# The first layer's triangle: row blocks outside, channels inside, with b kept on chip in fp16 parts

## The chip, the core and the metric

The kernel runs on one core of a Trainium2 chip. The metric is device time in microseconds (us) of one execution. TensorE (PE in the profile; PEld its weight loads), VectorE (DVE), ScalarE (ACT), GpSimd (POOL) and SyncE (SP, which here only issues DMAs) run their own instruction streams, each in order; they wait for each other by semaphores.

## The reference, cut to what matters

The input x is a pair tensor of 512 x 512 x 128, fp32. Two layers follow each other; both are residual and begin with a group normalisation. The change lies in the first layer:

```
a = sigmoid((x @ Wa1 + ba1) * (x @ Wa2 + ba2))        # 512 x 512 x 16
b = sigmoid((x @ Wb1 + bb1) * (x @ Wb2 + bb2))        # 512 x 512 x 16
g = sigmoid(x @ Wg + bg)
z = einsum('bikc,bkjc->bijc', a, b)                   # 16 products of 512 x 512 matrices
x = x + g * (layernorm(z over c) @ Wz + bz)
```

So each of the 16 channels c is one matrix product z[:, :, c] = a[:, :, c] @ b[:, :, c], and the layer norm then runs over the 16 channels of each pair (i, j). The second layer has a similar pair of triangles and is not touched.

## The kernel before

There are seven stages behind each other with a barrier between them: statistics, gates (writes a and b to the DRAM tensor ab_d, as [512, 32, 512] fp32), the triangle (stage 3, changed here), the first layer's output, and three stages of the second layer. Stage 3 reads ab_d and writes the normalised z as two fp16 parts (rounded value and rest) to z_d.

The products are made in fp16 parts: a value is the sum of high (the value rounded to fp16, by ScalarE) and rest (value minus high, by VectorE). One product of a row block of 128 rows i with all 512 columns j is 12 matmuls: 4 blocks of the sum index k, times three terms (high x high, high x rest, rest x high).

The channels are the outer loop and the four row blocks `ib` the inner one. Per channel, SyncE loads all of a[c] and all of b[c] (1 MB each) into a ring of three `raw` buffers (L617): the next a waits until a buffer's transposes are done, the next b until a buffer's rests are done. TensorE transposes a (`turn`, L637, four transposes of 128x128 for each of four units into `t_ps`). ScalarE makes high from `t_ps` and from `raw` (L670), VectorE makes rest (L733), both into `ab`, which has two buffers, so that channel c + 1 is prepared during the products of channel c. The lists ORDER and AFTER fix by hand in which order the 8 units of the next channel are placed between the products. TensorE's 12 matmuls write `z_ps` (L649). ScalarE copies channel 0 to `z` (L691); for the other channels VectorE subtracts channel 0 while it copies (`take`, L748). Channel 0 so serves as a base that makes the values small; its own slot is zeroed later. GpSimd adds up z (L722) and the squares that ScalarE makes (L678, L726) in `total` and `total2`.

After the last channel come, for each row block, the variance (L752, L755), the square root (L699), the zeroing (L759) and the reciprocal (L761), and then for each half of 8 channels: normalising (L767, VectorE), rounding (L705, ScalarE), the rest (L771, VectorE) and two stores of 1 MB (L621, L623). All of that stands behind the last product.

Of the kernel before, what the change touches and what calls it, by code (L numbers as in the profile page):

```python
# [11 lines left out]
P = 128  # L12
# [561 lines left out]
def stage3_triangle(nc, K, ab_d, z_d, N):  # L574
# [4 lines left out]
    RB, C, SLOTS = N // P, 16, 3  # L579
    UNITS, CHUNK = 2 * RB, C // 2  # L580
    AFTER = ((4, 5), (0, 1, 6), (2, 3, 7), ())
    ORDER = (4, 5, 0, 1, 6, 2, 3, 7)
    a_v = ab_d.rearrange("(b p) c k -> c p b k", p=P)
    b_v = ab_d.rearrange("(p b) c k -> c p b k", b=RB)
    z_v = z_d.rearrange("(h c) (b p) j -> h b p c j", h=2, p=P)
    with ExitStack() as stack:
        s = Scope(nc, stack, "s3")
        raw = s.sbuf("raw", [P, SLOTS, RB, N])
        ab = s.sbuf("ab", [P, 2, 2, 2, RB, N], FP16)
        z = s.sbuf("z", [P, C, RB, N])  # L590
        total, total2 = s.sbuf("total", [P, RB, N]), s.sbuf("total2", [P, RB, N])
        parts = ab[:].rearrange("p x m h k j -> p (x m h k) j").rearrange("p (x h c) j -> p x h c j", x=2, h=2)
        def square(c, n):

            return z[:, C - 1, 2 + n % 2, :] if c + 1 < C else raw[:, 2, n % 2, :]

        z_ps = s.psum("z_ps", [P, RB, BANK])
        t_ps = s.psum("t_ps", [P, 4, BANK])
        loaded, stored = s.sems("loaded", SLOTS), s.sems("stored", 2)
        turned, rounded, rest_ready, product, taken, squared, summed, summed2 = [  # L600
            s.sem(n) for n in ("turned", "rounded", "rest_ready", "product", "taken", "squared", "summed", "summed2")]
        zeroed, meant, scaled, var_ready, dev_ready, inverted, cleared, normed, z_rounded, z_split = [
            s.sem(n) for n in ("zeroed", "meant", "scaled", "var_ready", "dev_ready", "inverted", "cleared", "normed", "z_rounded", "z_split")]

        @block_of(nc)
        def _(block):
            @block.sync
            def _(sp):
                for n in range(2 * C):
                    c, m = n // 2, n % 2  # L610
                    before = n - SLOTS
                    if before >= 0 and before % 2 == 0:
                        sp.wait_ge(turned, RB * (before // 2 + 1))
                    elif before >= 0:
                        sp.wait_ge(rest_ready, UNITS * (before // 2 + 1))
                    src = (a_v[c], b_v[C + c])[m]
                    sp.dma_start(raw[:, n % SLOTS, :, :], src).then_inc(loaded[n % SLOTS], 16)  # L617
                for k in range(2 * RB):
                    ib, half = k // 2, slice(CHUNK * (k % 2), CHUNK * (k % 2) + CHUNK)
                    sp.wait_ge(z_rounded, k + 1)  # L620
                    sp.dma_start(z_v[0, ib][:, half, :], parts[:, k % 2, 0, :, :]).then_inc(stored[k % 2], 16)  # L621
                    sp.wait_ge(z_split, k + 1)
                    sp.dma_start(z_v[1, ib][:, half, :], parts[:, k % 2, 1, :, :]).then_inc(stored[k % 2], 16)  # L623
                for k in range(2):
                    sp.wait_ge(stored[k], RB * 32)

            @block.tensor
            def _(pe):
                def turn(c, q):

                    n = 2 * c
                    if q == 0:
                        pe.wait_ge(loaded[n % SLOTS], n // SLOTS * 16 + 16)
                    if c:
                        pe.wait_ge(rest_ready, UNITS * (c - 1) + ORDER.index(q) + 1)
                    for b in range(RB):
                        last = pe.transpose(t_ps[:, q, b * P:(b + 1) * P], raw[:, n % SLOTS, b, q * P:(q + 1) * P], K.ident[:])  # L637
                    last.then_inc(turned, 1)

                for q in range(RB):  # L640
                    turn(0, q)
                for c in range(C):
                    pe.wait_ge(rest_ready, UNITS * (c + 1))
                    for ib in range(RB):
                        if c:
                            pe.wait_ge(taken, RB * (c - 1) + (ib + 1))
                        terms = [(kb, a, b) for kb in range(RB) for a, b in ((0, 0), (0, 1), (1, 0))]
                        for m, (kb, a, b) in enumerate(terms):
                            last = pe.matmul(z_ps[:, ib, 0:N], ab[:, c % 2, 0, a, kb, ib * P:(ib + 1) * P], ab[:, c % 2, 1, b, kb, :],  # L649
                                             start=m == 0, stop=m == len(terms) - 1)  # L650
                        last.then_inc(product, 1)
                        if c + 1 < C and ib + 1 < RB:
                            for v in AFTER[ib + 1]:
                                if v < RB:
                                    turn(c + 1, v)

            @block.scalar
            def _(act):
                def round_high(c, v):
                    if c >= 2 and v == ORDER[0]:  # L660
                        act.wait_ge(product, RB * (c - 1))
                    if v < RB:
                        act.wait_ge(turned, RB * c + v + 1)
                        src = t_ps[:, v, 0:N]
                    else:
                        n = 2 * c + 1
                        if v == RB:
                            act.wait_ge(loaded[n % SLOTS], n // SLOTS * 16 + 16)
                        src = raw[:, n % SLOTS, v % RB, :]
                    act.activation(ab[:, c % 2, v // RB, 0, v % RB, :], src, ACT.Copy).then_inc(rounded, 1)  # L670

                def take_square(c, ib):

                    n = RB * (c - 1) + ib
                    act.wait_ge(taken, RB * c + ib + 1)
                    if n >= 2:
                        act.wait_ge(summed2, n - 1)
                    act.activation(square(c, n), z[:, c, ib, :], ACT.Square).then_inc(squared, 1)  # L678

                for v in ORDER:  # L680
                    round_high(0, v)
                for c in range(C):
                    for ib in range(RB):
                        if c + 1 < C:
                            for v in AFTER[ib]:
                                round_high(c + 1, v)
                        if c and ib:
                            take_square(c, ib - 1)
                        if c == 0:
                            act.wait_ge(product, ib + 1)  # L690
                            act.activation(z[:, 0, ib, :], z_ps[:, ib, 0:N], ACT.Copy).then_inc(taken, 1)  # L691
                    if c:
                        take_square(c, RB - 1)
                for ib in range(RB):
                    act.wait_ge(summed, RB * (C - 2) + ib + 1)
                    act.wait_ge(summed2, RB * (C - 1) - 1 + ib // 2)
                    act.activation(raw[:, 0, ib, :], total[:, ib, :], ACT.Square, scale=1.0 / C).then_inc(meant, 1)
                    act.wait_ge(var_ready, ib + 1)
                    act.activation(raw[:, 1, ib, :], total2[:, ib, :], ACT.Sqrt).then_inc(dev_ready, 1)  # L699

                def round_z(k):
                    act.wait_ge(normed, k + 1)
                    if k >= 2:
                        act.wait_ge(stored[k % 2], k // 2 * 32)
                    act.activation(parts[:, k % 2, 0, :, :], z[:, CHUNK * (k % 2):CHUNK * (k % 2) + CHUNK, k // 2, :],  # L705
                                   ACT.Copy).then_inc(z_rounded, 1)

                for k in range(2 * RB):
                    round_z(k)

            @block.gpsimd
            def _(pool):
                pool.memset(total[:], 0.0).then_inc(zeroed, 1)  # L713
                pool.memset(total2[:], 0.0).then_inc(zeroed, 1)
                pool.wait_ge(zeroed, 2)
                for c in range(1, C):
                    for ib in range(RB):
                        n = RB * (c - 1) + ib
                        pool.wait_ge(taken, RB * c + ib + 1)
                        if c > 1:  # L720
                            pool.wait_ge(summed, n - 3)
                        pool.tensor_tensor(total[:, ib, :], total[:, ib, :], z[:, c, ib, :], ALU.add).then_inc(summed, 1)  # L722
                        pool.wait_ge(squared, n + 1)
                        if c > 1:
                            pool.wait_ge(summed2, n - 3)
# [1117 lines left out]
```

## Time and profile before

| | us |
|---|---|
| median of 3 runs (4824.75 to 4827.78) | 4825.3 |
| the profiled execution | 4827.47 |
| its span, first to last instruction | 4825.7 |
| TensorE / VectorE / ScalarE / GpSimd busy in the span | 3997.2 / 3925.1 / 3395.2 / 2674.1 |

The granted TensorE clock is 0.975 in the mean over the span (1.00 is 2.4 GHz, 0.50 is 1.2 GHz). Stage 3 issues its first load at 943.45 us of the span, and stage 4 starts at 1254.05. A row of the view by groups reads: line, engine, operation, written tile <- read tiles, shapes, count | busy us in the stretch, mean ns of one | idle time of the engine before them, and what ended it. A row in order of time reads: start us, us, engine, line, what, and in square brackets the idle time before it.

### The profile page before, as it was taken

The page shows a single profiled execution, that of the slowest core. Times are in us where ns is not written, and L with a number is a line of the kernel's source. Part 1 is how long each engine was busy: PE and PEld are TensorE (multiplying, and loading weights), DVE is VectorE, ACT ScalarE, POOL GpSimd, SP SyncE. Part 2 cuts the span into 40 slices and gives each one's busy share as a digit, 9 for nine tenths or more (in the row PEclk, how much of TensorE's full clock was granted, in tenths as well). Part 3 has the DMA queues.
Part 4 walks back from the last instruction along what each step waited for, and adds up shares of the span by engine and source line. Part 5 has one row for each costly group of instructions (what it writes and reads, how often), then busy time and mean ns, then how long its engine had stood idle before and what let it go on. Part 6 is the DMA issues. An engine that isn't in the chain of part 4 may idle for free. (4 is left out here: it accounts for less than half of the span.)

```text
span 4825.7 us, 89597 instructions
## 1 busy us (share of the span) xinstructions
PE 3997.2 (83%) x26438; PEld 2240.6 (46%) x26438; DVE 3925.1 (81%) x5450; ACT 3395.2 (70%) x4840; POOL 2674.1 (55%) x1428
## 2 busy tenths in 40 slices
PE   0007888795599999889999999979999978888888
PEld 0004444452366666545555555545554434444444
DVE  5787777678888888989999999867779987777777
ACT  2337777654577777768888888746667768888887
POOL 0000000085488888757778777843334418888887
PEclk9999999997799999989999999999999989999999
DMA  9997888753999999969999999876679869999999
GB/s 367 416 385 247 296 299 301 241 175 105 307 399 390 390 391 391 393 215 316 315 315 318 311 313 318 276 263 222 224 237 308 302 213 362 407 405 404 402 404 362
DMA packets 700625, 1532.70 MB, mean 318 GB/s; under 512 B 32976, under 2 KB 50832, under 8 KB 698128
## 3 DMA queue, kind: packets, MB, share of 16 engines
q1 hardware_dynamic: 563696, 1263.31, 73.0%
q10 hardware_dynamic: 136864, 268.59, 14.5%
q8 instruction: 33, 0.54, 0.0%
q14 instruction: 32, 0.26, 0.0%
HBM read 1009.59 MB, written 522.19 MB: 317 GB/s over the span
## 5 line engine op out<-in xcount | busy, mean ns | idle before, releaser
L1762 POOL TENSOR_TENSOR s_oT<-s_gated,s7in_x1t 128x1024 f32<-128x1024 f32 x256 | 689.4, 2699 | 218.5 <-DVE s_gated L1681 213.6
L976 POOL TENSOR_TENSOR s_x1T<-s_gz,s_xT 128x512 f32<-128x512 f32 x512 | 653.4, 1276 | 126.6 <-DVE s_gz L942 122.0
L1428 PE MATMUL s_y_ps<-s_ab 128*128 128x512 f16 x3072 | 678.4, 379 | 1.8 <-DVE s_ab L1499 1.8
L1133 POOL TENSOR_TENSOR s_low<-s_xc,s_high 128x1024 f16<-128x1024 f32 x256 | 547.8, 2140 | 237.4 <-ACT s_high L1094 235.9
L873 PE MATMUL s_g_ps<-s_xT,s_Wg 128*128 128x512 f32 x1024 | 523.3, 593 | 0.0
L713 POOL MEMSET s_total<- 128x2048 f32 x1 | 1.8, 1810 | 936.2 <-POOLq L41 936.2
L903 ACT ACTIVATE s_g<-s_g_ps,s_bg 128x512 f32<-128x512 f32 x512 | 352.0, 688 | 173.1 <-PE s_g_ps L873 173.1
L1681 DVE SCALAR_TENSOR_TENSOR s_gated<-s_p_ps,k_po_bias,s_gate 128x1024 f32<-128x1024 f32 x256 | 328.7, 1284 | 177.2 <-ACT s_gate L1718 145.7
L1428 PEld LDWEIGHTS s_y_ps<-s_ab 128*128 128x128 f16 x3072 | 300.4, 98 | 343.4 <-issue 2.0
L548 DVE SCALAR_TENSOR_TENSOR s_low<-s_x_ps,k_gn_scale,s_high 128x1024 f16<-128x1024 f32 x256 | 328.5, 1284 | 161.0 <-ACT s_high L498 160.9
L942 DVE SCALAR_TENSOR_TENSOR s_gz<-s_z_ps,k_z_bias,s_g 128x512 f32<-128x512 f32 x512 | 384.4, 751 | 88.8 <-ACT s_g L903 86.6
L1099 ACT ACTIVATE s_gate<-s_g_ps,k_gi_bias 128x1024 f32<-128x1024 f32 x256 | 284.3, 1110 | 200.7 <-PE s_g_ps L1268 200.4
L1402 POOL TENSOR_TENSOR s_at<-s_at,s_mask 128x1024 f32<-128x1024 f32 x64 | 151.1, 2360 | 460.6 <-DMA s_bt<-h_d 265.6
L1718 ACT ACTIVATE s_gate<-s_g_ps,k_go_bias 128x1024 f32<-128x1024 f32 x256 | 286.0, 1117 | 148.0 <-PE s_g_ps L1627 134.8
L863 PEld LDWEIGHTS s_x_ps<-k_ident,s_xt 128*128 128x128 f32 x2048 | 257.1, 141 | 274.8 <-issue 268.3
L1172 DVE BATCH_NORM_STATS2 s_stats<-s_x_ps 128x6 f32<-128x256 f32 x1024 | 364.1, 418 | 7.8 <-PE s_x_ps L1243 7.1
L1201 DVE SCALAR_TENSOR_TENSOR s_h<-s_p_ps,k_pi_bias,s_gate 128x1024 f32<-128x1024 f32 x256 | 328.2, 1282 | 46.8 <-PE s_p_ps L1268 32.2
L933 DVE BATCH_NORM_STATS2 s_stats<-s_x1T 128x512 f32 (+1 forms) x512 | 349.8, 683 | 0.2 <-POOL s_x1T L976 0.2
L498 ACT ACTIVATE s_high<-s_x_ps,k_gn_scale 128x1024 f16<-128x1024 f32 x256 | 285.2, 1114 | 74.3 <-PE s_x_ps L454 73.6
L307 DVE BATCH_NORM_STATS2 s_stats<-s_xt 128x512 f32 x416 | 248.5, 682 | 81.1 <-DMA s_xt<-in_x 81.1
L863 PE MATMUL s_x_ps<-k_ident,s_xt 128*128 128x128 f32 x2048 | 308.5, 274 | 6.5 <-DVE s_bg L929 6.5
L1194 DVE TENSOR_TENSOR s_xc<-s5in_xt,s_r_ps 128x1024 f32<-128x1024 f32 x256 | 310.2, 1212 | 4.3 <-PE s_r_ps L1259 3.0
(225 smaller groups left out, 9506.7 us busy)
## 6 DMA issues: line engine op xcount, KB each, us to landing
s2in_xt<-in_x SPq DMA_DIRECT2D x128, 1024.0 KB, 8.5
s_xt<-in_x SPq DMA_DIRECT2D x256, 512.0 KB, 8.4
x_d<-s_x1T ACTq DMA_DIRECT2D x128, 1024.0 KB, 9.6
s5in_xt<-x_d SPq DMA_DIRECT2D x128, 1024.0 KB, 9.2
h_d<-s_h SPq DMA_DIRECT2D x128, 1024.0 KB, 6.9
s7in_x1t<-x_d SPq DMA_DIRECT2D x128, 1024.0 KB, 14.0
out<-s_ot ACTq DMA_DIRECT2D x128, 1024.0 KB, 9.3
s_mask_b<-mask_d SPq DMA_DIRECT2D x128, 512.0 KB, 4.8
```

The lines of the kernel that those rows point to most:

```text
L548: dve.scalar_tensor_tensor(low[:, g % GROUPS, 2 * h:2 * h + 2, :], x_ps[:, (2 * g + h) % SLOTS, :, 0:N], K.gn_scale[:], high[:, g % GROUPS ...
L863: last = pe.transpose(x_ps[:, i % 4, q * P:(q + 1) * P], xt[:, i // U, i % U, q, :], K.ident[:])
L873: pe.matmul(g_ps[:, i % 2, 0:N], Wg[:], xT[:, i % 8, :], start=True, stop=True).then_inc(g_prod, 1)
L903: act.activation(g[:, i % 2, :], g_ps[:, i % 2, 0:N], ACT.Sigmoid, bias=bg[:]).then_inc(sig, 1)
L933: dve.bn_stats(stats[:, bass.ds(r * ROWS + i, 1), :].rearrange("p a s -> p (a s)"), x1T[:, i // U, i % U, :]).then_inc(counted, 1)
L942: dve.scalar_tensor_tensor(gz[:, i % 4, :], z_ps[:, i % 2, 0:N], K.z_bias[:], g[:, i % 2, :], ALU.add, ALU.mult).then_inc(mixed, 1)
L976: pool.tensor_tensor(x1T[:, i // U, i % U, :], gz[:, i % 4, :], xT[:, i % 8, :], ALU.add).then_inc(added, 1)
L1133: pool.tensor_tensor(low[:, n % 4, :, :], xc[:, n % 4, :, :], high[:, n % 4, :, :], ALU.subtract).then_inc(rest_ready, 1)
L1172: last = dve.bn_stats(stats[:, row // 16 % 2, row % 2, row // 2 % BLOCK, a, :], x_ps[:, row % 2, 2 * a * P:(2 * a + 2) * P].rearrange("p ( ...
L1428: last = pe.matmul(y_ps[:, ib, 0:N], ab[:, u % 2, 0, a, kb, ib * P:(ib + 1) * P], ab[:, u % 2, 1, b, kb, :], start=m == 0, stop=m == len(t ...
L1681: dve.scalar_tensor_tensor(gated[:, n % 4, :, :], p_ps[:], K.po_bias[:], gate[:, n % 2, :, :], ALU.add, ALU.mult).then_inc(mixed, 1)
L1762: pool.tensor_tensor(oT[:, n % 4, :, :], gated[:, n % 4, :, :], x1t[:, n // 2, 2 * (n % 2):2 * (n % 2) + 2, :], ALU.add).then_inc(added, 1)
```

## The change

The loops are exchanged: the row block n of 128 rows is the outer loop and the channel c the inner one, 64 steps g = 16 n + c. All 16 channels of b are loaded, rounded and kept in fp16 parts (`b`) during block 0; a is loaded in pieces of 128 rows of one channel (256 KB), three deep. `z` becomes a ring of 24 slots of one block and channel; the landing place of b, `raw_b`, is in the eight slots that block 0 doesn't use. Block n is normalised in chunks of two channels during the channels of block n + 1 (the steps are in the tables NORM, ROUND and SPLIT), the last block after the last product. The normalising reads the reciprocal deviation from PSUM (`dev_ps`). There is one `square`, `total` and `total2` buffer of one block in place of one for each block, and GpSimd starts each block's sums with copies instead of adding to zeroed tiles. The diff is cut to what each engine issues in which order:

```diff
+    RB, C, ZS, CHUNK, TERMS = N // P, 16, 24, 2, ((0, 0), (0, 1), (1, 0))
+    CHUNKS, LATER, STEPS = C // CHUNK, C - 1, RB * C
+    NORM, ROUND, SPLIT = (4, 5, 7, 8, 10, 11, 13, 14), (5, 6, 8, 9, 11, 12, 14, 15), (6, 7, 9, 10, 12, 13, 15, 16)
...
+        b = s.sbuf("b", [P, C, 2, RB, N], FP16)
+        raw_a = s.sbuf("raw_a", [P, 3, N])
+        a = s.sbuf("a", [P, 3, 2, N], FP16)
+        z = s.sbuf("z", [P, ZS, N])
+        raw_b = z[:, C:C + 2 * RB, :].rearrange("p (s b) j -> p s b j", b=RB)
+        square = s.sbuf("square", [P, N])
+        z_ps = s.psum("z_ps", [P, 3, BANK])
+        t_ps = s.psum("t_ps", [P, 3, BANK])
...
             def _(sp):
+                for g in range(STEPS):
+                    if g < C:
+                        if g >= 2:
+                            sp.wait_ge(b_rest, g - 1)
+                        sp.dma_start(raw_b[:, g % 2, :, :], b_v[C + g]).then_inc(b_loaded[g % 2], 16)
+                    if g >= 3:
+                        sp.wait_ge(turned, g - 2)
+                    sp.dma_start(raw_a[:, g % 3, :], a_v[g // C, g % C]).then_inc(a_loaded[g % 3], 16)
+                    for n, k in due(g - 6, SPLIT):
+                        store(n, k)
...
             def _(pe):
+                for g in range(STEPS):
+                    if g + 2 < STEPS:
+                        turn(g + 2)
+                    pe.wait_ge(a_rest, g + 1)
+                    pe.wait_ge(b_rest, min(g, C - 1) + 1)
+                    before = g - 3
+                    if before >= 0 and before % C == 0:
+                        pe.wait_ge(based, before // C + 1)
+                    elif before >= 0:
+                        pe.wait_ge(taken, later(before))
...
             def _(act):
+                def round_b(c):
+                    act.wait_ge(b_loaded[c % 2], c // 2 * 16 + 16)
+                    act.activation(b[:, c, 0, :, :], raw_b[:, c % 2, :, :], ACT.Copy).then_inc(b_rounded, 1)
...
+                round_b(0)
+                for g in range(2):
+                    round_a(g)
+                for g in range(STEPS):
+                    n, c = g // C, g % C
+                    if g + 2 < STEPS:
+                        round_a(g + 2)
+                    if g + 1 < C:
+                        round_b(g + 1)
+                    if c == 0:
+                        take_base(g)
+                    if g and (g - 1) % C:
+                        take_square(g - 1)
+                    if n and c == 1:
+                        mean_square(n - 1)
+                    if n and c == 2:
+                        deviation(n - 1)
+                    for block_n, k in due(g, ROUND):
+                        round_z(block_n, k)
...
             def _(dve):
+                def normalize(n, k):
+                    dve.wait_ge(inverted, n + 1)
+                    dve.wait_ge(cleared, n + 1)
+                    part = chunk_of(n, k)
+                    dve.tensor_tensor(part, part, dev_ps[:, 0:N].rearrange("p (a j) -> p a j", a=1).to_broadcast([P, CHUNK, N]), ALU.mult).then_inc(normed, 1)
...
+                rest_b(0)
+                for g in range(2):
+                    rest_a(g)
+                for g in range(STEPS):
+                    n, c = g // C, g % C
+                    if g + 2 < STEPS:
+                        rest_a(g + 2)
+                    if g + 1 < C:
+                        rest_b(g + 1)
+                    if c:
+                        take(g)
+                    if n and c == 1:
+                        variance(n - 1)
+                    if n and c == 2:
+                        clear_base(n - 1)
+                    if n and c == 3:
+                        invert(n - 1)
+                    for block_n, k in due(g, SPLIT):
+                        split(block_n, k)
+                    for block_n, k in due(g, NORM):
+                        normalize(block_n, k)
...
-        K.gn_mean, K.gn_scale, K.gn_shift = s.sbuf("gn_mean", [P, 1]), s.sbuf("gn_scale", [P, 1]), s.sbuf("gn_shift", [P, 1])
+        columns = s.sbuf("gn", [P, 4])
+        K.gn_mean, K.gn_scale, K.gn_shift = columns[:, 0:1], columns[:, 1:2], columns[:, 2:3]
```

In it, `turn(g)` waits for a_loaded of g, for rest_a(g - 3) and transposes; `round_a(g)` waits for turn(g) and for product g - 3; `rest_a` and `rest_b` wait for the rounding of the same piece; `take(g)` waits for product g; `store` waits for z_rounded and z_split of its chunk, and `round_z(j)` for the two stores of chunk j - 2. GpSimd's two adds of step g wait for `taken` and `squared` of that step, and `take_square(g)` for the add of the square before.

## Rows read from the trace of the kernel before

**Rows 1.** Busy time by stretch: us, busy and count by engine, clock, DMA share, GB/s.
```profile
965.00:1147.00 182.00, 182.00 (x960) 97.30 (x959) 138.53 (x175) 98.19 (x177) 157.97 (x112) 1.00 0.49 157
...
1163.00:1254.00 91.00, 0.00 (x0) 0.00 (x0) 83.54 (x24) 29.13 (x9) 0.00 (x0) 0.50 0.55 185
```
**Rows 2.** Busy time by stretch, one channel in the middle of stage 3.
```profile
1051.00:1063.10 12.10, 12.10 (x65) 6.51 (x64) 9.98 (x14) 7.10 (x13) 11.56 (x8) 1.00 0.54 173
```
**Rows 3.** Order of time, start of stage 3.
```profile
943.45 51.77 SPq L617 DMA_DIRECT2D s_raw<-ab_d  x11
...
951.00 3.68 PE L637 MATMUL s_t_ps<-k_ident,s_raw 128*128 128x128 f32 x16 [13.18 <-DMA s_raw<-ab_d]
953.68 1.15 ACT L670 ACTIVATE s_ab<-s_raw 128x512 f16<-128x512 f32 x2 [14.38 <-DMA s_raw<-ab_d]
...
959.30 4.10 PE L649 MATMUL s_z_ps<-s_ab 128*128 128x512 f16 x12 [4.62 <-DVE s_ab L733]
```
**Rows 4.** Order of time, the last take, the last store, and stage 4's start.
```profile
1152.86 0.69 DVE L748 TENSOR_TENSOR s_z<-s_z_ps,s_z 128x512 f32<-128x512 f32 x1 [1.90 <-PE s_z_ps L649]
...
1246.73 0.37 SPq L623 DMA_DIRECT2D z_d<-s_ab  x1
1254.05 6.92 POOL L968 MEMSET s_zt<- 64x8192 f16 x1 [96.50 <-POOLq L41]
```
**Rows 5.** SyncE's waits in stage 3: us in total, times, longest us.
```profile
SPq L617 <- PE s_t_ps L637: 126.8, 15, 9.6
...
SPq L617 <- DVE s_ab L733: 39.6, 14, 4.0
```
**Rows 6.** Transfers: line 617's landings, then others (count, KB, median us to landing).
```profile
DMA to landing us min/median/max: 5.2/5.7/11.7
...
z_d<-s_ab SPq DMA_DIRECT2D x16, 1024.0 KB, 4.5
s_mask<-mask_d SPq DMA_DIRECT2D x1, 512.0 KB, 4.0
...
k_Wg<-in_Wg SPq DMA_DIRECT2D x1, 64.0 KB, 2.0
```
**Rows 7.** Busy time by stretch, PE alone, in the first transposes: clock, DMA, GB/s last.
```profile
951.00:952.00 1.00, 1.00 (x5) 0.50 1.04 393
```
**Rows 8.** Groups of instructions by line and shape, 930 to 1260 us.
```profile
L722 POOL TENSOR_TENSOR s_total<-s_total,s_z 128x512 f32<-128x512 f32 x60 | 78.2, 1303 | 41.1 <-DVE s_z L748 41.0
...
L733 DVE TENSOR_TENSOR s_ab<-s_raw,s_ab 128x512 f16<-128x512 f32 x64 | 73.1, 1162 | 37.1 <-ACT s_ab L670 37.1
L748 DVE TENSOR_TENSOR s_z<-s_z_ps,s_z 128x512 f32<-128x512 f32 x60 | 41.0, 683 | 25.7 <-PE s_z_ps L649 25.7
L733 DVE TENSOR_TENSOR s_ab<-s_t_ps,s_ab 128x512 f16<-128x512 f32 x64 | 40.8, 677 | 4.8 <-ACT s_ab L670 4.8
...
L678 ACT ACTIVATE s_z<-s_z 128x512 f32<-128x512 f32 x56 | 35.4, 632 | 61.7 <-DVE s_z L748 61.5
L767 DVE TENSOR_TENSOR s_z<-s_z,s_total 128x4096 f32<-128x4096 f32 x8 | 34.9, 4409 | 0.0
L771 DVE TENSOR_TENSOR s_ab<-s_z,s_ab 128x4096 f16<-128x4096 f32 x8 | 34.9, 4401 | 0.0
...
L670 ACT ACTIVATE s_ab<-s_t_ps 128x512 f16<-128x512 f32 x64 | 34.7, 594 | 14.8 <-PE s_t_ps L637 14.7
...
L705 ACT ACTIVATE s_ab<-s_z 128x4096 f16<-128x4096 f32 x8 | 28.9, 3618 | 49.6 <-DVE s_z L767 49.6
L761 DVE RECIPROCAL s_total<-s_raw 128x512 f32<-128x512 f32 x4 | 13.2, 3294 | 0.0
```
**Rows 9.** Line 733 reading SBUF, 965 to 1147 us: duration ns min/median/max.
```profile
L733 DVE TENSOR_TENSOR s_ab<-s_raw,s_ab x58: 681/1186/1792, 965.8 to 1139.9; 128x512 f16<-128x512 f32 x58
```
**Rows 10.** Order of time, VectorE and GpSimd near 1127 us.
```profile
1126.79 1.27 POOL L722 TENSOR_TENSOR s_total<-s_total,s_z 128x512 f32<-128x512 f32 x1
1127.41 1.19 DVE L733 TENSOR_TENSOR s_ab<-s_raw,s_ab 128x512 f16<-128x512 f32 x1
1128.02 1.73 POOL L726 TENSOR_TENSOR s_total<-s_total,s_z 128x512 f32<-128x512 f32 x1
```

More of the change, by code:

```diff
@@ L584, in stage3_triangle @@
     b_v = ab_d.rearrange("(p b) c k -> c p b k", b=RB)
-    z_v = z_d.rearrange("(h c) (b p) j -> h b p c j", h=2, p=P)
+    z_v = z_d.rearrange("(h c) (n p) j -> h n p c j", h=2, p=P)
     with ExitStack() as stack:
         s = Scope(nc, stack, "s3")
[L588 to L603, printed above, removed]
@@ L605, in _, with later, chunk_of, due @@
+        normed, z_rounded, z_split = s.sem("normed"), s.sem("z_rounded"), s.sem("z_split")
+        def later(g):
+            return LATER * (g // C) + g % C
+        def chunk_of(n, k):
+            first = (C * n + CHUNK * k) % ZS
+            return z[:, first:first + CHUNK, :]
+        def due(step, table):
+            return [(step // C - 1 - e, k) for e in (0, 1) for k, at in enumerate(table)
+                    if at == step % C + C * e and 0 <= step // C - 1 - e < RB - 1]
         @block_of(nc)
@@ L608, in _ @@
             def _(sp):
[L609 to L625, printed above, removed]
+                def store(n, k):
+                    j = CHUNKS * n + k
+                    channels = slice(CHUNK * k, CHUNK * k + CHUNK)
+                    for h, ready in ((0, z_rounded), (1, z_split)):
+                        sp.wait_ge(ready, j + 1)
+                        sp.dma_start(z_v[h, n][:, channels, :],
+                                     parts[:, j % 2, h, :, :]).then_inc(stored[j % 2], 16)
@@ L627, in _ @@
+                for step in range(STEPS - 6, STEPS + 1):
+                    for n, k in due(step, SPLIT):
+                        store(n, k)
+                for k in range(CHUNKS):
+                    store(RB - 1, k)
+                for x in range(2):
+                    sp.wait_ge(stored[x], RB * CHUNKS // 2 * 32)
             @block.tensor
             def _(pe):
[L629 to L637, printed above, removed]
-                    last.then_inc(turned, 1)
@@ L640, in _, with turn @@
[L640 to L655, printed above, removed]
+                def turn(g):
+                    pe.wait_ge(a_loaded[g % 3], g // 3 * 16 + 16)
+                    if g >= 3:
+                        pe.wait_ge(a_rest, g - 2)
+                    for q in range(RB):
+                        last = pe.transpose(t_ps[:, g % 3, q * P:(q + 1) * P], raw_a[:, g % 3, q * P:(q + 1) * P], K.ident[:])
+                    last.then_inc(turned, 1)
@@ new lines, in _ @@
+                for g in range(2):
+                    turn(g)
+                for g in range(STEPS):
[8 more added lines that the diff above has]
+                        pe.wait_ge(taken, later(before))
+                    terms = [(q, x, y) for q in range(RB) for x, y in TERMS]
+                    for m, (q, x, y) in enumerate(terms):
+                        last = pe.matmul(z_ps[:, g % 3, 0:N], a[:, g % 3, x, q * P:(q + 1) * P], b[:, g % C, y, q, :],
+                                         start=m == 0, stop=m == len(terms) - 1)
+                    last.then_inc(product, 1)
@@ L657, in _ @@
             @block.scalar
             def _(act):
[L659 to L670, printed above, removed]
@@ L694, in _ @@
[L694 to L706, printed above, removed]
@@ L708, in _, with round_a @@
-                for k in range(2 * RB):
-                    round_z(k)
+                def round_a(g):
+                    act.wait_ge(turned, g + 1)
+                    if g >= 3:
+                        act.wait_ge(product, g - 2)
+                    act.activation(a[:, g % 3, 0, :], t_ps[:, g % 3, 0:N], ACT.Copy).then_inc(a_rounded, 1)
+                def round_b(c):
+                    act.wait_ge(b_loaded[c % 2], c // 2 * 16 + 16)
+                    act.activation(b[:, c, 0, :, :], raw_b[:, c % 2, :, :], ACT.Copy).then_inc(b_rounded, 1)
@@ new lines, in take_base, with take_square @@
+                def take_base(g):
+                    n = g // C
+                    act.wait_ge(product, g + 1)
+                    if n == 1:
+                        act.wait_ge(b_rest, C)
+                    if n >= 2:
+                        act.wait_ge(z_split, CHUNKS * (n - 2) + (ZS - C) // CHUNK + 1)
+                    act.activation(z[:, g % ZS, :], z_ps[:, g % 3, 0:N], ACT.Copy).then_inc(based, 1)
+                def take_square(g):
+                    m = later(g)
+                    act.wait_ge(taken, m)
+                    if m >= 2:
+                        act.wait_ge(summed2, m - 1)
+                    act.activation(square[:], z[:, g % ZS, :], ACT.Square).then_inc(squared, 1)
@@ L711, in _ @@
+                take_square(STEPS - 1)
+                mean_square(RB - 1)
+                deviation(RB - 1)
+                for k in range(CHUNKS):
+                    round_z(RB - 1, k)
             @block.gpsimd
             def _(pool):
[L713 to L725, printed above, removed]
-                        pool.tensor_tensor(total2[:, ib, :], total2[:, ib, :], square(c, n), ALU.add).then_inc(summed2, 1)
+                for g in range(STEPS):
+                    n, c, m = g // C, g % C, later(g)
+                    if c == 0:
+                        continue
+                    pool.wait_ge(taken, m)
+                    if c == 1:
+                        if n:
+                            pool.wait_ge(meant, n)
+                        pool.tensor_copy(total[:], z[:, g % ZS, :]).then_inc(summed, 1)
+                        pool.wait_ge(squared, m)
+                        if n:
+                            pool.wait_ge(dev_ready, n)
+                        pool.tensor_copy(total2[:], square[:]).then_inc(summed2, 1)
+                    else:
+                        pool.wait_ge(summed, m - 1)
+                        pool.tensor_tensor(total[:], total[:], z[:, g % ZS, :], ALU.add).then_inc(summed, 1)
+                        pool.wait_ge(squared, m)
+                        pool.wait_ge(summed2, m - 1)
+                        pool.tensor_tensor(total2[:], total2[:], square[:], ALU.add).then_inc(summed2, 1)
@@ L774, in _, with rest_a @@
-                for ib in range(RB):
-                    variance(ib)
-                for ib in range(2):
-                    invert(ib)
-                for ib in range(RB):
-                    normalize(2 * ib)
-                    normalize(2 * ib + 1)
-                    if ib + 2 < RB:
-                        invert(ib + 2)
-                    split(2 * ib)
-                    split(2 * ib + 1)
+                def rest_a(g):
+                    dve.wait_ge(a_rounded, g + 1)
+                    dve.tensor_tensor(a[:, g % 3, 1, :], t_ps[:, g % 3, 0:N], a[:, g % 3, 0, :], ALU.subtract).then_inc(a_rest, 1)
@@ new lines, in rest_b, with take @@
+                def rest_b(c):
+                    dve.wait_ge(b_rounded, c + 1)
+                    dve.tensor_tensor(b[:, c, 1, :, :], raw_b[:, c % 2, :, :], b[:, c, 0, :, :], ALU.subtract).then_inc(b_rest, 1)
+                def take(g):
+                    n = g // C
+                    dve.wait_ge(product, g + 1)
+                    dve.wait_ge(based, n + 1)
+                    if g >= ZS:
+                        dve.wait_ge(z_split, (g - ZS) // CHUNK + 1)
+                    elif n:
+                        dve.wait_ge(b_rest, C)
+                    dve.tensor_tensor(z[:, g % ZS, :], z_ps[:, g % 3, 0:N], z[:, C * n % ZS, :], ALU.subtract).then_inc(taken, 1)
@@ new lines, in split @@
+                def split(n, k):
+                    j = CHUNKS * n + k
+                    dve.wait_ge(z_rounded, j + 1)
+                    dve.tensor_tensor(parts[:, j % 2, 1, :, :], chunk_of(n, k), parts[:, j % 2, 0, :, :], ALU.subtract).then_inc(z_split, 1)
+                rest_b(0)
+                for g in range(2):
+                    rest_a(g)
+                for g in range(STEPS):
+                    n, c = g // C, g % C
[15 more added lines that the diff above has]
+                        normalize(block_n, k)
@@ L787, in stage4_layer0 @@
+                for block_n, k in due(STEPS, SPLIT):
+                    split(block_n, k)
+                last = RB - 1
+                variance(last)
+                clear_base(last)
+                invert(last)
+                normalize(last, 0)
+                for k in range(1, CHUNKS):
+                    normalize(last, k)
+                    split(last, k - 1)
+                split(last, CHUNKS - 1)
 def stage4_layer0(nc, K, x, z_d, x1_d, N, ahead):
```

99 lines of the change are left out of this document (37 added, 62 removed).

## The prediction

> **What bounds the kernel now.** The change touches one stage, the first layer's triangle. I read the busy time by stretch first. From 965 to 1147 us TensorE is busy for all of it, while from 1163 to 1254 it does nothing and VectorE is busy for 83.54 of 91 us [rows 1]. So the stage has two parts with two limits: 16 channels at TensorE's pace, then a normalising tail at VectorE's pace. The stretch of one channel gives the pace of the first part: 12.10 us, four row blocks of 12 matmuls and 4 transposes, so 3.02 us for one block of one channel [rows 2]. The order of time gives the ends: the last "take" (VectorE subtracting the base from z_ps) starts at 1152.86, the last store is issued at 1246.73 and stage 4 starts at 1254.05 [rows 4]. SyncE issues the first load at 943.45 [rows 3], so the stage takes 310.6 us, and 101.2 of it lie behind the last take's start.
>
> **What the change removes.** TensorE's work is the same: 64 steps of 12 matmuls and 4 transposes. The tail shrinks, because three of four blocks are normalised beside the next block's products. What is new is the pace of the first block, in which all 16 channels of b must be loaded (1 MB each), rounded and kept.
>
> **Block 0, the term that decides.** I write t(c) for the end of VectorE's rest_b(c). Follow the four queues; each is in order.
> - SyncE, turn g: it waits for rest_b(g-2), issues the 1 MB load of b(g), and only then the 256 KB load of a(g). That it stands still for VectorE is nothing new: it did so 14 times before, for up to 4.0 us [rows 5]; but now the load of a is behind that wait.
> - TensorE, step g-2: turn(g) comes first, so it waits for a(g).
> - ScalarE, step g-2: round_a(g), then round_b(g-1). The second is queued behind the first, although b(g-1) landed long ago.
> - VectorE, step g-2: rest_a(g), then rest_b(g-1).
>
> So t(g-1) cannot come before t(g-2) + the load of b(g) and a(g) + turn(g) + round_a(g) + round_b(g-1) + rest_b(g-1), for g = 2 to 15. The three-deep ring for a and the two-deep ring for b hide nothing: each step pays a whole load. The price of one round:
> - Loads. A 1 MB load of this tensor lands 5.2 us after its issue at best, 5.7 in the median [rows 6]; queued loads follow at 2.7 us per MB (the first consumer starts at 951.00, the second load's at 953.68) [rows 3], which is 0.7 for 256 KB. 5.2 to 5.7 and 0.7, with 0.1 for SyncE to wake: 6.3 us (6.0 to 6.9).
> - turn(g): 16 transposes took 3.68 us in a stretch whose granted clock was 0.50, the lower of the two levels [rows 3, 7], so 0.92 for 4. In block 0 TensorE idles most of a step, so I take this; at the upper level it would be half, 0.46.
> - round_a: 0.59 [rows 8].
> - round_b, 2048 elements: between 0.632 for 512 and 3.618 for 4096 [rows 8] lies a slope of 0.833 ns per element, so 1.91.
> - rest_b, 2048 elements: between 0.681 for 512 undisturbed [rows 9] and 4.401 for 4096 [rows 8], slope 1.038, so 2.28. rest_a (0.68) runs beside round_b, the products beside the load.
> - Handing over between engines: 0.1.
>
> Sum 6.3 + 0.9 + 0.6 + 1.9 + 2.3 + 0.1 = 12.1 us a round, bounds 10.6 (5.2 for the loads, with a(g) landing 0.2 behind b(g), 0.46 for the turn, no handing over) and 13.2 (6.9 for the loads, and half an add of GpSimd in the way, 0.5). GpSimd's adds fall into the load's time, so I charge no wait here. TensorE alone would want 3.02.
>
> A page speaks on the load term. The Trainium skill (DMA: Bandwidth & Descriptors, section "Anatomy of one DMA — SWDGE (gpsimd) path") gives a fit of 2.0 us fixed plus bytes over 436 GB/s. For 1.25 MB that is an estimate of 5.0 us; the rows have 5.2 for 1 MB alone. By the page a round would be 1.3 shorter and the time about 18 us less; the rows decide.
>
> Start of the block: b(0) is now first in the queue and lands at 951.0 as the first load did; 1.9 + 2.3 later t(0) = 955.2, 11.8 us after the stage's start. Fourteen rounds, 169.4 us, lead to t(14). a(16) and a(17) wait for no b, so rest_b(15) is done 4 to 5 us after t(14), beside matmul(14): that is 4.1 us at the low clock [rows 3], turn(17) 0.5, matmul(15) 2.6 (3.02 less a turn): 7.2 us to the end of product 15.
>
> **Blocks 1 to 3.** TensorE wants 16 x 3.02 = 48.4 us a block. VectorE's count: 16 x (rest_a 0.677 + take 0.683) = 21.8 [rows 8]; three short operations at 0.68 = 2.0; one reciprocal 3.29 [rows 8]; 8 normalisings and 8 splits of 1024 elements, 0.681 + 512 x 1.038 ns = 1.21 each, 19.4 (before: 4.4 for 4096 either way [rows 8]). Sum 46.5, no lower bound on the time since TensorE's 48.4 is above it. On top come waits for GpSimd. The row pair of VectorE and GpSimd shows them: a subtraction with both inputs in SBUF, started at 1127.41, took 1.19 and ended 0.54 after GpSimd's add ended at 1128.06; GpSimd's next add, started at 1128.02, took 1.73 in place of 1.27 [rows 10]. They take turns. The subtraction that reads PSUM has a mean of 0.677 beside the same adds, that from SBUF 1.162 [rows 8]. So rest_a, take and normalising (one input in PSUM) pay nothing, and the 8 splits do: from nothing to a whole add of 1.27, hence a block between 48.4 and 46.5 + 10.2 = 56.7. GpSimd is nearly full itself: 15 pairs of adds at 1.27 are 38.1, with 8 splits that shut it out 47.8, so half an add, 0.6, is the value nearest to the row: 46.5 + 4.8 = 51.3, and I take 51. Three blocks: 153 us (145 to 168). Three banks of z_ps let VectorE fall two steps behind, so uneven steps (the one with the reciprocal) average out. Loads of a and stores of parts are issued some three steps ahead, 9 us, against landings of 2.0 for 64 KB, 4.0 for 512 KB and 4.5 for 1 MB [rows 6]; they are covered. ScalarE has 16 x (0.594 + 0.632) + 8 x 1.06 + 2.4, about 31 of 51 us.
>
> **The tail.** After product 63: take 0.7, GpSimd's last adds (some behind, so up to 5 us; at least 0.63 for the square and 1.27 for an add), variance 1.4, Sqrt 0.65, reciprocal 3.3: about 10. Then 8 chunks of normalise and split at 2.42: 19.4, or up to 23, since round_z waits for the stores of two chunks before; I take 21. From the last store's issue to stage 4 it was 7.3 with 1 MB at 4.5, so 2.8 beside the landing [rows 4, 6]; 256 KB between 2.0 and 4.0 gives about 6. Tail 37 (31 to 40).
>
> **Sum.** 11.8 + 169.4 + 7.2 + 153 + 37 = 378.4 us in place of 310.6: 68 us more. The profiled execution took 4827.5 us, so 4895.4 by its own time; the median of the runs is 2.2 lower, so 4893. The bounds: 11.8 + 148 + 6 + 145 + 31 = 342 gives +31 (4857); 11.8 + 185 + 8 + 168 + 40 = 413 gives +102 (4927). The stages behind read z_d in the same layout and start when the stage ends; I charge them nothing. The three gn columns cut from one tile are read by the same instructions: nothing.
>
> **Rivals.**
> - *Block 0 runs at the pace of VectorE and GpSimd, and the kernel is faster.* If the loads ran ahead, a step would cost rest_b 2.28 plus a pair of adds 2.54 that take turns with it, 4.8 us. 14 x (4.8 - 12.1) = -102, so 34 us under before: 4791. For it: 393 GB/s while loads are queued [rows 7], so the data themselves want 3.4 us a step. Against it: SyncE's queue held loads behind VectorE in the kernel before too [rows 5], and the load of a stands behind that wait in the code. The point from which it decides: a round below 12.1 - 68/14 = 7.2 us, for which the loads would have to cost 1.4. Chance 4%.
> - *a(g) doesn't wait for the bytes of b(g).* Then it lands as a 256 KB load by itself, about 2.9 us between the rows' 2.0 and 4.0 [rows 6], 0.6 after b's issue; a round is 9.4 and the time 68 - 38 = 30 us above before: 4855. Against it: the first two loads landed 2.7 us apart [rows 3]. Chance 9%. The Trainium skill (DMA: Bandwidth & Descriptors, "Queues, rings and completion order") says that completion is not in order per issuing engine, which would allow this; the same section lets each engine take descriptors in ring order, which the rows' 2.7 us agree with.
> - *VectorE and GpSimd bind blocks 1 to 3.* At 56.7 a block, 17 us more: 4910. For it: GpSimd's 47.8 of 48.4. Against it: five of eight splits have a step without normalising behind them, to catch up. Chance 12%.
> - *The loss in block 0 and the gain in the tail cancel*: within 0.2% (9.7 us, about what a measurement of this kernel can tell from no change), which wants a round near 7.2. Chance 2%.
>
> **How the numbers follow.** Forecast 73%, the rivals 4, 9, 12 and 2%. The likeliest time is 4893. The range takes in the second and third rival and the bounds: 4852 to 4928. Faster 0.04, same 0.02, slower 0.94.
>
> **What would show it.** In the changed profile: rest_b of neighbouring channels 12 us apart in block 0; TensorE idle there for some 60% of the time, its transposes waiting for the DMA of raw_a about 6 us, 14 times; ScalarE's round_a waiting for TensorE as often; a low granted clock there; after it steps of 3.0 to 3.3 us; splits well above 1.21 in the mean and normalisings at 1.2; about 37 us from the last product to stage 4. Wrong: rest_b starts 5 us apart, SyncE not waiting for VectorE, or TensorE's steps in blocks 1 to 3 above 3.6 us.

## The result and the profile after

The changed kernel takes 4876.65 us in the median of 4 runs (4876.49 to 4876.76); the kernel before took 4825.97 beside it. The ratio is 1.0103, with a 95% interval of 1.009 to 1.0116: 50.7 us slower. The forecast was 4893, with 4852 to 4928 as its range.

The busy time by stretch shows where. The columns are those of [rows 1]: the stretch and its length, busy us and count of PE, PEld, DVE, ACT and POOL, granted clock, DMA share, GB/s. The stretches are the 14 rounds of block 0, then blocks 1, 2 and 3, then what follows the last product. Blocks 1 to 3 are each counted from the start of their second product; the first three products behind the rounds, from 1120.54 to 1131.19, lie in no stretch.

```profile
955.03:1120.54 165.51, 76.60 (x232) 34.46 (x232) 50.65 (x44) 41.07 (x43) 46.53 (x24) 0.66 0.34 116
1131.19:1179.60 48.41, 48.41 (x258) 26.25 (x257) 43.97 (x49) 28.70 (x44) 41.69 (x30) 1.00 0.53 156
1179.60:1228.00 48.40, 48.40 (x258) 26.24 (x257) 46.18 (x52) 27.29 (x43) 43.95 (x31) 1.00 0.59 175
1228.00:1272.40 44.40, 44.40 (x231) 23.26 (x229) 42.19 (x48) 23.67 (x37) 40.04 (x28) 1.00 0.49 150
1272.40:1307.88 35.48, 0.00 (x1) 0.00 (x0) 28.61 (x24) 12.28 (x14) 7.42 (x5) 0.55 0.44 148
```

In block 0 no engine is busy for half of the time and the DMA engines have a share of 0.34: nothing is full, so it is a chain of waits. In blocks 1 to 3 TensorE is busy for all of it, beside the normalising of the block before. The tail behind the last product is 35.5 us; before, 101.2 us lay behind the last take's start. The stage's first load and stage 4's start:

```profile
945.47 0.65 SPq L634 DMA_DIRECT2D s_z<-ab_d  x1
...
1307.88 6.92 POOL L1031 MEMSET s_zt<- 64x8192 f16 x1 [28.06 <-POOLq L41]
```

So the stage takes 362.4 us.

One round of block 0 in order of time (start us, us, engine, line, what; in brackets the idle time before it and what ended it):

```profile
966.84 0.55 SPq L634 DMA_DIRECT2D s_z<-ab_d  x1
967.43 0.62 SPq L637 DMA_DIRECT2D s_raw_a<-ab_d  x1
972.69 0.71 PEld L655 LDWEIGHTS s_t_ps<-k_ident,s_raw_a 128*128 128x128 f32 x4 [6.90 <-DMA s_raw_a<-ab_d]
...
973.60 3.69 PE L672 MATMUL s_z_ps<-s_b,s_a 128*128 128x512 f16 x12
973.85 0.60 ACT L682 ACTIVATE s_a<-s_t_ps 128x512 f16<-128x512 f32 x1 [6.92 <-PE s_t_ps L655]
974.34 1.90 ACT L686 ACTIVATE s_b<-s_z 128x2048 f16<-128x2048 f32 x1
974.48 0.69 DVE L774 TENSOR_TENSOR s_a<-s_t_ps,s_a 128x512 f16<-128x512 f32 x1 [7.66 <-ACT s_a L682]
976.27 2.29 DVE L778 TENSOR_TENSOR s_b<-s_z,s_b 128x2048 f16<-128x2048 f32 x1 [1.11 <-ACT s_b L686]
...
978.59 0.55 SPq L634 DMA_DIRECT2D s_z<-ab_d  x1
```

(`raw_b` lies in `z`, so the load of b is `s_z<-ab_d`.) From the issue of b(g) to the next one it is 11.75 us: 5.85 until a(g) has landed and its turn starts, 1.16 for the turn up to round_a's start, 0.49 to round_b's start, 1.93 to rest_b's start, 2.29 for rest_b, and SyncE issues the next b at once. The first rest_b starts at 952.74, the fifteenth at 1118.25: 14 rounds of 11.82. SyncE's waits (us in total, times, longest) answer to [rows 5]; 14 waits for rest_b have grown from 39.6 to 144.6 us:

```profile
SPq L634 <- DVE s_b L778: 144.6, 14, 10.7
SPq L637 <- PE s_t_ps L655: 85.1, 38, 4.7
```

### The profile page after: what moved, and what is told of

Same layout as the page of the kernel before. It is cut to its first block and busy times, and to the rows that moved or that the text cites. A ratio compares the mean times of both kernels' runs of the same rounds, so it can differ in the third digit from the quotient of the medians.

```text
span 4875.0 us, 89868 instructions
## 1 busy us (share of the span) xinstructions
PE 4023.5 (83%) x26438; PEld 2249.4 (46%) x26438; DVE 3904.5 (80%) x5450; ACT 3393.9 (70%) x4816; POOL 2688.9 (55%) x1426
## 5 line engine op out<-in xcount | busy, mean ns | idle before, releaser
L548 DVE SCALAR_TENSOR_TENSOR s_low<-s_x_ps,k_gn,s_high 128x1024 f16<-128x1024 f32 x256 | 328.5, 1283 | 161.1 <-ACT s_high L498 161.1
L498 ACT ACTIVATE s_high<-s_x_ps,k_gn 128x1024 f16<-128x1024 f32 x256 | 285.2, 1114 | 74.9 <-PE s_x_ps L454 74.8
```

## The experiments

Theory: in block 0 the load of a(g) stands in SyncE's queue behind the wait for rest_b(g-2), while ScalarE and VectorE have round_b(g-1) and rest_b(g-1) queued behind a(g). So each channel pays one load and all that follows it, one after the other. The rival is that the loads, or the work of the engines itself, need that time in any order.

**SyncE's order: a(g) ahead of b(g)'s wait** (e1_a_first)

```diff
+                    if g >= 3:
+                        sp.wait_ge(turned, g - 2)
+                    if g >= 2:
+                        sp.dma_start(raw_a[:, g % 3, :], a_v[g // C, g % C]).then_inc(a_loaded[g % 3], 16)
                     if g < C:
                         if g >= 2:
                             sp.wait_ge(b_rest, g - 1)
                         sp.dma_start(raw_b[:, g % 2, :, :], b_v[C + g]).then_inc(b_loaded[g % 2], 16)
...
```

> Only SyncE's order is changed: from g = 2 the load of a(g) is issued ahead of the wait for rest_b(g-2) and of the load of b(g). My theory (a round of block 0 is one chain, because the load of a(g) is queued behind the wait for rest_b(g-2), so that each round pays load 5.9, turn 1.15, round_a 0.5, round_b 1.9 and rest_b 2.3, 11.8 in all): a(g) is then behind rest_b(g-3), the same chain spans two channels, rest_b starts 5.9 us apart, and the kernel takes 4876.7 - 14 x 5.9 = 4794 us, which is also less than before. Rival (the round is the work of the engines and of the loads, which has to be done in any order): rounds above 10 us and 4860 or more.

Measured: 4796.66 us, ratio to before 0.9941 (0.9924 to 0.9957). The 16 rest_b start from 953.01 to 1042.60, 5.97 us apart. The view of their line (count: duration ns min/median/max, first and last start):

```profile
L781 DVE TENSOR_TENSOR s_b<-s_z,s_b x16: 2291/2292/2294, 953.0 to 1042.6; 128x2048 f16<-128x2048 f32 x16
```

The chain is right in kind and in size (5.9 expected), and the same amount of work and bytes takes half the time once two instructions have changed places.

**ScalarE's and VectorE's order: b(g+1) ahead of a(g+2)** (e2_b_first)

```diff
-                    if g + 2 < STEPS:
-                        round_a(g + 2)
                     if g + 1 < C:
                         round_b(g + 1)
+                    if g + 2 < STEPS:
+                        round_a(g + 2)
...
                     if g + 1 < C:
                         rest_b(g + 1)
+                    if g + 2 < STEPS:
+                        rest_a(g + 2)
```

> SyncE's order stays; ScalarE does round_b(g+1) ahead of round_a(g+2) and VectorE rest_b(g+1) ahead of rest_a(g+2). My theory: rest_b(g-1) no longer stands behind a(g); the chain closes over two channels (load 5.9, turn 1.15, round_a 0.6, a square 0.6, round_b 1.9, rest_b 2.3 = 12.4), 6.2 us a round, 4876.7 - 14 x 5.6 = 4798 us: nearly the same as the edit of SyncE's order, from the other end of the chain. Rival (the chain closes elsewhere, in SyncE's own queue or in the loads): rounds of 10 us or more and 4855 or more.

Measured: 4811.86 us, ratio 0.9967 (0.9954 to 0.9979). The chain opens from this end too, but rounds are 6.84 us in the mean (952.90 to 1055.51), not 6.2. They come in pairs, 3.4 and 10.4. VectorE and TensorE in order of time in the long one:

```profile
991.41 1.12 PE L655 MATMUL s_t_ps<-k_ident,s_raw_a 128*128 128x128 f32 x4 [6.11 <-DMA s_raw_a<-ab_d]
992.32 4.10 PE L672 MATMUL s_z_ps<-s_b,s_a 128*128 128x512 f16 x12
...
996.46 0.69 DVE L788 TENSOR_TENSOR s_z<-s_z_ps,s_z 128x512 f32<-128x512 f32 x1 [2.58 <-PE s_z_ps L672]
997.06 2.28 DVE L778 TENSOR_TENSOR s_b<-s_z,s_b 128x2048 f16<-128x2048 f32 x1
```

In this order rest_b stands behind the take of the step before, and that waits for a product that is itself behind the turn of a(g) and takes 4.10 us (the granted clock from 991.41 to 996.46 is 0.64; at 1.00 a product takes 2.75). round_b had ended at 995.47, so the detour over TensorE costs some 1.6 us in each pair. I had left the take out of this chain.

**SyncE's order, one more step: a(g+1) ahead of b(g)'s wait** (e3_a_ahead)

```diff
...
+                    elif g < C:
+                        if g == 2:
+                            load_a(2)
+                        load_a(g + 1)
+                        sp.wait_ge(b_rest, g - 1)
+                        sp.dma_start(raw_b[:, g % 2, :, :], b_v[C + g]).then_inc(b_loaded[g % 2], 16)
...
```

> SyncE's order alone, one more step ahead: a(g+1) is issued ahead of the wait for rest_b(g-2) and of the load of b(g). My theory: a is out of the chain; what is left is the two-deep ring of b (load 5.2, round_b 1.9, rest_b 2.3 = 9.5 for two channels, 4.8 a round), beside VectorE's rest_b and GpSimd's two adds, which take turns (2.24 + 2.44 = 4.7): rounds of 4.8 to 5.3, 4876.7 - 14 x 6.8 = 4782 (4775 to 4788). Rival (a's place in the queue is not what counts; b's ring alone sets the round in the first edit too): no faster than that one, 4790 to 4800.

Measured: 4782.81 us, ratio 0.9911 (0.9895 to 0.9928): 43 us less than before, and the fastest of the kernels that leave nothing out. rest_b starts 5.01 us apart (951.89 to 1027.11):

```profile
L787 DVE TENSOR_TENSOR s_b<-s_z,s_b x16: 2292/2293/2689, 951.9 to 1027.1; 128x2048 f16<-128x2048 f32 x16
```

**Both loads behind the wait, a(g) first** (e4_same_wait)

```diff
                     if g < C and g >= 2:
                         sp.wait_ge(b_rest, g - 1)
...
                     sp.dma_start(raw_a[:, g % 3, :], a_v[g // C, g % C]).then_inc(a_loaded[g % 3], 16)
+                    if 2 <= g < C:
+                        sp.dma_start(raw_b[:, g % 2, :, :], b_v[C + g]).then_inc(b_loaded[g % 2], 16)
...
```

> a(g) still waits for rest_b(g-2), but is issued ahead of b(g) instead of behind it. My theory: the chain stays, its load is a(g) alone, 2.9 us as in blocks 1 to 3 in place of 5.9, so rounds of 8.8 us and 4876.7 - 14 x 3.0 = 4835 us. Rival (bytes of b in front of a don't count, since loads of one queue share the engines): a lands about 5 us after its issue, rounds above 11 us, 4868 or more.

Measured: 4830.35 us, ratio 1.0012 (1.0003 to 1.0022). Rounds of 8.48 us (953.42 to 1072.07 in 14). In order of time, a round's loads and the turn that waits for them:

```profile
981.40 0.33 SPq L637 DMA_DIRECT2D s_raw_a<-ab_d  x1
981.78 0.55 SPq L639 DMA_DIRECT2D s_z<-ab_d  x1
...
984.19 0.66 PE L657 MATMUL s_t_ps<-k_ident,s_raw_a 128*128 128x128 f32 x4 [4.03 <-DMA s_raw_a<-ab_d]
```

2.8 us from a's issue to its use, with 1 MB of b right behind it; in the changed kernel, with b in front, it is 5.26 from a's issue and 5.85 from b's. The place behind b's bytes and the wait are two parts of the chain: without b in front a round is 3.3 us shorter (8.48 against 11.82; 3.0 had been expected), and with a ahead of the wait too, as in the first edit, another 2.5 (5.97).

**Each split of blocks 0 to 2 made twice** (e5_split_twice)

```diff
                     for block_n, k in due(g, SPLIT):
+                        spare(block_n, k)
+                        dve.wait_ge(spared, CHUNKS * block_n + k + 1)
                         split(block_n, k)
...
```

(`spare` is the same subtraction into the same tile.)

> The changed kernel with each split of blocks 0 to 2 (during blocks 1 to 3) made twice by VectorE, the second over the first. My theory: these blocks run at TensorE's pace, 48.4 us, but VectorE has only some 2 us idle in each, so that 8 more splits of 1.13 to 2.3 us (the wait for GpSimd's adds included) make VectorE the bound: 7 to 16 us more per block, 4898 to 4925 us in all. Rival (VectorE is far from the bound and its waits would fill with the extra work): under 4882.

Measured: 4913.63 us, 37 us above the changed kernel (ratio to before 1.0177, 1.016 to 1.0194). Its block 2, from the last take of block 1 to its own last take, by the view by stretch:

```profile
1193.49:1253.12 59.63, 49.64 (x253) 25.73 (x252) 59.27 (x60) 27.21 (x43) 49.58 (x31) 0.98 0.48 142
```

VectorE is busy for 59.27 of 59.63 us: with 8 more splits it is the bound, 11.2 us above TensorE's 48.4. They added 13.1 us to VectorE's busy time (46.18 in the changed kernel's block 2) and 11.2 to the block. So the changed kernel had some 2 us of room on VectorE in each block, and no more.

**What holds the better order at 5 us a round.** Two suspects lay at nearly one height: the ring of b (load, round_b and rest_b of a slot, two channels deep) and VectorE taking turns with GpSimd. Three kernels take away the one, the other, and both, all with a(g+1) ahead of b(g).

```diff
+                    for h in range(2):
+                        dve.wait_ge(b_rounded, 2 * c + h + 1)
+                        dve.tensor_tensor(b[:, c, 1, 2 * h:2 * h + 2, :], raw_b[:, (2 * c + h) % 4, :, :],
+                                          b[:, c, 0, 2 * h:2 * h + 2, :], ALU.subtract).then_inc(b_rest, 1)
```

(e6_halves: loads and round_b are halved in the same way)

```diff
+                        w = 16 if n == 0 else N
+                        pool.tensor_tensor(total[:, 0:w], total[:, 0:w], z[:, g % ZS, 0:w], ALU.add).then_inc(summed, 1)
...
+                        pool.tensor_tensor(total2[:, 0:w], total2[:, 0:w], square[:, 0:w], ALU.add).then_inc(summed2, 1)
```

(e7_no_adds, which keeps 16 of the 512 columns of block 0's adds and leaves out the sums of the others; e8_halves_no_adds has both edits)

> The order with a(g+1) ahead of b(g), and b loaded, rounded and subtracted in halves of 512 KB in a ring of four. If the ring of b alone sets that order's round of 5.0 us, the halves shorten it to what TensorE, ScalarE or the bytes want, 3.4 to 3.6: 4783 - 15 x 1.4 = 4762. My theory: VectorE's rest_b and GpSimd's adds, which take turns (2.24 + 2.44 = 4.7 us a round), lie right below it: 4783 - 15 x 0.3 = 4778.

> The order with a(g+1) ahead of b(g), with GpSimd's adds of block 0 cut to 16 of 512 columns (the sums of the other columns are left out). My theory: the ring of b (load 5.2, round_b 1.9, rest_b 2.3, two channels in 9.5) still wants 4.8 us a round, so the gain is at most 0.2 a round: 4780 (4777 to 4785). Rival (taking turns with GpSimd is what sets the round): 3.6 to 4.0 us a round, 4762 to 4768.

> Both at once: b in halves and GpSimd's adds of block 0 cut to 16 columns (the sums of the other columns are left out). My theory: two limits of nearly the same height are gone together, and the round falls to VectorE's 2.24 + 0.6 + 0.6 or the bytes' 3.4 (1.25 MB at 390 GB/s), 3.5 to 3.8 us: 4783 - 15 x 1.35 = 4763 (4758 to 4768). Rival (a third limit, such as ScalarE or the low clock, holds the round near 4.7): 4775 or more.

| kernel | us | block 0: first to 15th take, us a step |
|---|---|---|
| a(g+1) ahead | 4782.81 | 66.97 / 14 = 4.78 |
| with halves | 4787.71 | 69.83 / 14 = 4.99 |
| without GpSimd's adds in block 0 | 4787.33 | 66.61 / 14 = 4.76 |
| halves, and without the adds | 4774.48 | 56.05 / 14 = 4.00 |

The ratios to before are 0.9911, 0.9915, 0.9918 and 0.9886, and the four intervals overlap, so the steps are the better measure; the runs of the last kernel (4770 to 4777 us) do all lie below those of the two above it (4783 to 4791). Neither edit alone shortens a step, both together take off 0.8: there are two limits, as expected. The sizes were off: all three times lie above what was expected (4778, 4780 and 4763 us). For one thing, the halves made the step a little longer. From 960 to 1020 us, VectorE's groups in e6_halves and in e8_halves_no_adds (line, engine, operation, count | busy us, mean ns | idle before):

```profile
L796 DVE TENSOR_TENSOR s_b<-s_z,s_b 128x1024 f16<-128x1024 f32 x26 | 46.9, 1838 | 1.9 <-ACT s_b L703 1.9
```

```profile
L797 DVE TENSOR_TENSOR s_b<-s_z,s_b 128x1024 f16<-128x1024 f32 x29 | 35.3, 1236 | 5.0 <-ACT s_b L703 5.0
```

The same half of rest_b takes 1.84 us beside the adds and 1.24 without them. The view by stretch of e6_halves:

```profile
960.00:1020.00 60.00, 45.06 (x193) 20.84 (x192) 58.06 (x49) 37.26 (x49) 32.39 (x22) 0.89 0.81 264
```

VectorE is busy for 58.06 of these 60 us; with b in one piece it is 43.37. Cut in two, rest_b can wait for GpSimd twice. In one piece it had mostly run ahead of the add (2.29 us in 13 of its 16 cases with a(g+1) ahead, 2.69 at most), and the add waited instead, where it held up nothing: without the adds a step is 4.76 against 4.78. So at least a part of the 4.99 comes from the cut itself; how high the second limit lies with rest_b in one piece was not measured. And with both limits gone a step is 4.00, not 3.5 to 3.8. The view by stretch of that kernel points to the next limit:

```profile
960.00:1020.00 60.00, 50.08 (x240) 25.25 (x241) 51.61 (x58) 44.66 (x58) 12.52 (x25) 0.96 0.94 314
```

The DMA engines are busy for 0.94 of it at 314 GB/s, and from 975 us on for 0.98 at 333 GB/s; 1.25 MB (1.31 million bytes) a step at 333 GB/s are 3.9 us. I had reckoned with 390 GB/s. That the loads are the limit is read from these shares; no run tries it.

## Why the prediction was right

It had the sign, the place and the mechanism, and was 16 us too high; more than half of that is one term, blocks 1 to 3. Its terms for the stage, against the changed kernel's trace:

| term | predicted us | measured us |
|---|---|---|
| start to t(0) | 11.8 | 9.6 (945.47 to 955.03) |
| 14 rounds | 169.4 | 165.5 (11.82 each, 12.1 predicted) |
| to the end of product 15 | 7.2 | 7.5 (to 1128.03) |
| blocks 1 to 3 | 153 | 144.4 (to 1272.40) |
| tail | 37 | 35.5 (to 1307.88) |
| stage | 378.4 | 362.4; before 310.6 |

So the stage is 51.8 us longer. It starts 2.0 later than before, and the later stages are 4.5 shorter (3567.1 us from stage 4's start to the end of the span, 3571.7 before); among the other kernels here, whose later stages are the same, that stretch is 3562.4 to 3574.4, so I put it down to the spread of one execution.

- *Block 0 is a chain of one load and four operations.* Right, by three edits that open it or shorten it at different places: 5.9 predicted and 5.97 measured, 8.8 and 8.48, 4.8 to 5.3 and 5.01. The fourth, in ScalarE's and VectorE's order, opened it too, but was mis-sized by 0.6 a round, for the reason shown.
- *Loads, 6.3 us.* 5.85. The landings of b's loads are 5.0 to 5.4 us, without the longer ones that lifted the median of [rows 6] to 5.7; from before's trace I could not tell loads of a from loads of b. The term was 0.45 too high and the next one 0.24 too low, which partly cancels in the round.
- *The turn, 0.92.* 1.16 from its start to round_a's start. The lower level was the right choice: the granted clock is 0.50 in the four transposes of the round shown (972.69 to 973.60).
- *round_b 1.91 and rest_b 2.28.* 1.90 and 2.29: two sizes and a straight line were enough.
- *No charge for GpSimd in block 0.* Right. GpSimd's add of the squares takes the loss, 2.86 us in place of 1.27 at the last of the 14 rounds, with time to spare:

```profile
1118.25 2.29 DVE L778 TENSOR_TENSOR s_b<-s_z,s_b 128x2048 f16<-128x2048 f32 x1 [1.11 <-ACT s_b L686]
1118.82 2.86 POOL L768 TENSOR_TENSOR s_total<-s_total,s_square 128x512 f32<-128x512 f32 x1 [7.79 <-ACT s_square L702]
```

- *Blocks 1 to 3 at 51 us.* This is the term that was mis-sized: 48.1 us, TensorE's own pace, which was the lower bound given. VectorE's groups in block 2, from 1179.6 to 1228 us, answer to [rows 8]:

```profile
L814 DVE TENSOR_TENSOR s_parts<-s_z,s_parts 128x1024 f16<-128x1024 f32 x9 | 15.6, 1735 | 0.0
L774 DVE TENSOR_TENSOR s_a<-s_t_ps,s_a 128x512 f16<-128x512 f32 x16 | 10.8, 675 | 0.0
L788 DVE TENSOR_TENSOR s_z<-s_z_ps,s_z 128x512 f32<-128x512 f32 x15 | 10.2, 679 | 2.1 <-PE s_z_ps L672 2.1
L809 DVE TENSOR_TENSOR s_z<-s_z,s_dev_ps 128x1024 f32<-128x1024 f32 x8 | 9.7, 1206 | 0.0
...
```

The durations were right: normalising takes 1.206 (1.21 predicted), so with one input in PSUM it doesn't wait, and a split 1.735 here and 1.79 in the mean from 1128 to 1272 us, a wait of 0.5 to 0.6 where I took 0.6. With 5.0 us for the four groups not shown they add up to 51.3, just what was predicted (with one split more and one take fewer than a block has). But durations don't add up to time on this engine. In order of time:

```profile
1195.95 1.21 DVE L809 TENSOR_TENSOR s_z<-s_z,s_dev_ps 128x1024 f32<-128x1024 f32 x1
1197.08 0.68 DVE L774 TENSOR_TENSOR s_a<-s_t_ps,s_a 128x512 f16<-128x512 f32 x1
1197.68 0.68 DVE L788 TENSOR_TENSOR s_z<-s_z_ps,s_z 128x512 f32<-128x512 f32 x1
1198.28 1.57 DVE L814 TENSOR_TENSOR s_parts<-s_z,s_parts 128x1024 f16<-128x1024 f32 x1
```

From start to start an operation of 0.68 takes 0.60, and one of 1.21 takes 1.13. Over some 50 operations a block that is 4 us, most of the way from 51.3 down to the 46.2 busy of 48.4 us that block 2 shows. The experiment with the doubled splits shows that the rival of VectorE as the bound was 2 us a block away.
- *The tail, 37.* 35.5, of which VectorE is busy for 28.61: normalise and split take 1.13 to 1.2 each from start to start.
- *Start, 11.8.* 9.6: the first load of b lands 5.3 us after its issue, where the first load of the kernel before took 7.5. That one was a load of a, with 1 MB of b right behind it; here it is a load of b with 256 KB of a behind. Both are issued 3.75 us after SyncE has issued stage 2's last store, so that store is not the difference; what is was not tried.

## What to carry to other kernels

Read a new schedule queue by queue, and follow one piece of data round until the chain closes on itself: a ring of three buffers hides nothing when the refill of its next buffer stands behind another wait in the same queue. Here two instructions in SyncE's program were worth 80 us, and the exchange of loops paid only once that chain was opened, most of all by the order of the loads (4782.81 against 4825.50 before). Add up an engine like VectorE here by the time from start to start, not by the durations of its operations; and before cutting an operation in pieces, see who takes turns with it, since each piece can wait again.

## What was not expected of the hardware

- A 256 KB load is used 2.8 us after its issue with 1 MB queued behind it, and 5.3 us after it (5.85 after b's issue) with 1 MB queued in front: on this queue the load issued first was served first in both orders.
- In the profile VectorE's operations overlap by some 0.08 us: 0.60 from start to start at a duration of 0.68.
- With both other limits gone, the loads of block 0 ran at 314 GB/s and a DMA share of 0.94 (333 and 0.98 from 975 us on), not at the 393 GB/s of [rows 7]. The loads there were of a and b, 1 MB each; here they are pieces of 256 and 512 KB. Which of that lowers the rate stays open.
